# Two column states per GpSimd instruction: 128x1024 instead of 128x512 in turns 2 and 3

## The reference

```python
def step(state, xs):
    d_t, B_t, C_t, u_t = xs
    dA = jnp.exp(d_t[..., None] * A)
    state = state * dA + (d_t * u_t)[..., None] * B_t[:, None, :]
    y_t = jnp.einsum('ben,bn->be', state, C_t)
    return (state, y_t)
```

## Time and profile before

| | |
|---|---|
| median of 3 runs | 1370.07 us (1369.11 to 1371.49) |
| profiled execution, time | 1370.06 us |
| its span in the profile | 1368.3 us |
| TensorE busy | 1313.6 us, 96% |
| VectorE busy | 967.9 us, 71% |
| ScalarE busy | 623.3 us, 46% |
| GpSimd busy | 572.6 us, 42%, 317 instructions |
| TensorE's granted clock, mean | 0.991 of full speed |

### The profile page before, as it was taken

One profiled execution on the slowest core, in us unless ns is written; L12 is line 12 of the kernel. 1 busy time (PEld: TensorE's weight loads), 2 busy tenths in 40 slices (PEclk: granted clock), 3 DMA queues, 4 the chain that ended last, 5 costly groups with the idle time before them and its releaser, 6 DMA issues.

```text
span 1368.3 us, 17588 instructions
## 1 busy us (share of the span) xinstructions
PE 1313.6 (96%) x6018; PEld 1036.5 (76%) x6018; DVE 967.9 (71%) x1074; ACT 623.3 (46%) x1016; POOL 572.6 (42%) x317
## 2 busy tenths in 40 slices
PE   7899799999999999999999899999999899999999
PEld 4455478777777778888888778888888788888887
DVE  6899867899999776699999666699999523211111
ACT  6888366666565345544444135554443121111111
POOL 0000545788898421566765111566674211111111
PEclk8999999999999999999999999999999999999999
DMA  6211676776667755655555756555555665555552
GB/s 222 93 54 62 208 286 245 270 262 236 225 245 268 284 202 196 197 189 184 173 187 187 276 186 202 201 194 189 168 194 160 210 214 186 184 184 184 184 187 89
DMA packets 92301, 269.16 MB, mean 197 GB/s; under 512 B 11633, under 2 KB 11761, under 8 KB 91841
## 3 DMA queue, kind: packets, MB, share of 16 engines
q1 hardware_dynamic: 86912, 261.01, 55.7%
q10 hardware_dynamic: 5312, 7.16, 1.5%
HBM read 210.20 MB, written 57.93 MB: 196 GB/s over the span
## 4 chain that ended last, share of the span: by engine, by line
PE 76%; DVE 15%; issue 6%; ACT 2%; DMA 0%; DVEq 0%; ACTq 0%; POOL 0%
PE ps_hg L526 24%; PE ps_h L526 21%; PE ps_y L526 15%; DVE st L1278 8%; PE ps_y L707 8%; PE ps_mid L605 4%; DVE st L1269 2%; DVE y_rows L1289 2%; PE ps_mid L567 1%; PE ps_mid L526 1%; PE ps_y L549 1%; ACT dA L932 0%; DVE acc L1435 0%; DMA in_w<-in_in_wT_dram 0%; PE ps_mid L582 0%
## 5 line engine op out<-in xcount | busy, mean ns | idle before, releaser
L1597 POOL TENSOR_TENSOR h_lo<-h_tmp,h_hi 128x512 fp32r<-128x512 f32 x128 | 238.0, 1863 | 520.5 <-ACT h_hi L1007 458.2
L526 PE MATMUL ps_h<-x_hi,w_split 128*128 128x512 f32 x1024 | 344.9, 399 | 1.6 <-ACT x_hi L969 0.9
L526 PE MATMUL ps_hg<-x_hi,wg_split 128*128 128x512 f32 x1024 | 342.2, 395 | 0.6 <-DVE h_tmp L1442 0.6
L1278 DVE TENSOR_TENSOR_SCAN st<-dA,st 128x1024 f32<-128x1024 f32 x128 | 325.0, 2549 | 0.0
L1442 DVE TENSOR_TENSOR h_tmp<-h_tmp,ps_hg 128x512 f32<-128x512 f32 x128 | 88.1, 688 | 283.9 <-PE ps_hg L526 281.4
L526 PE MATMUL ps_y<-w_split,h_hi 128*128 128x512 f32 x1024 | 254.5, 396 | 0.0
L1007 ACT ACTIVATE h_hi<-h_tmp 128x512 fp32r<-128x512 f32 x128 | 80.6, 630 | 328.7 <-DVE h_tmp L1442 328.7
L526 PEld LDWEIGHTS ps_h<-x_hi,w_split 128*128 128x128 f32 x1024 | 193.2, 189 | 42.8 <-issue 2.9
L526 PEld LDWEIGHTS ps_hg<-x_hi,wg_split 128*128 128x128 f32 x1024 | 192.4, 188 | 40.4 <-issue 1.0
L526 PEld LDWEIGHTS ps_y<-w_split,h_hi 128*128 128x128 f32 x1024 | 188.1, 188 | 37.6
L1001 ACT ACTIVATE h_tmp<-ps_h 128x512 f32<-128x512 f32 x128 | 76.2, 595 | 293.2 <-PE ps_h L526 291.7
(11 more groups left out here) (161 smaller groups left out, 1298.6 us busy)
## 6 DMA issues: line engine op xcount, KB each, us to landing
w_split<-split_scratch SPq DMA_DIRECT2D x192, 512.0 KB, 5.5
wg_split<-split_scratch SPq DMA_DIRECT2D x96, 512.0 KB, 4.6
split_scratch<-w_split SPq DMA_DIRECT2D x64, 512.0 KB, 4.5
b_all<-xd_scratch SPq DMA_DIRECT2D x64, 256.0 KB, 4.1
split_scratch<-wg_split SPq DMA_DIRECT2D x32, 512.0 KB, 3.0
w_raw<-in_W_dram SPq DMA_DIRECT2D x14, 1024.0 KB, 7.4
wg_raw<-in_Wg_dram SPq DMA_DIRECT2D x7, 1024.0 KB, 9.4
dA<-in_x_dram SPq DMA_DIRECT2D x4, 1024.0 KB, 8.5
```

Of the source, the lines that this page charges most:

```text
L526: mm = pe.matmul(out_, lhs[a], rhs[c], start=first and q == 0, stop=last and q == len(sides) - 1)
L1278: dve.tensor_tensor_scan(flat[1], flat[0], flat[1], 0.0, ALU.mult, ALU.add).then_inc(scan_done, 1)
L1597: pool.tensor_tensor(h_lo[:, j, :], h_tmp[j % 2][:], h_hi[:, j, :].bitcast(F32), ALU.subtract).then_inc(hl_ready, 1)
```

## The change

In `column_state`, the two 128x512 multiplies of a part become one of 128x1024, with C's row repeated over the two tiles by a broadcast access pattern, and the two adds become one of 128x1024. The semaphores rise by 2 per instruction rather than by 1 twice. The waits on GpSimd's own semaphores are for the whole part.

```diff
                 used, odd = NC * (m - 2) + k, COLS[k] % 2
                 pool.wait_ge(cc_ld[used % 2], 16 * (used // 2 + 1))
                 pool.wait_ge(scan_done, 2 * (DS * m + COLS[k]) + part // 2 + 1)
-                for et in (part, part + 1):
-                    pool.tensor_tensor(st[odd][:, et, :], st[odd][:, et, :], c_all[used % 2], ALU.mult).then_inc(col_scaled, 1)
+                two = slice(part, part + 2)
+                by = c_all[used % 2].rearrange("p (a l) -> p a l", a=1).broadcast_to([P, 2, L])
+                pool.tensor_tensor(st[odd][:, two], st[odd][:, two], by, ALU.mult).then_inc(col_scaled, 2)
                 pool.wait_ge(ud_ready, T * m)
-                for et in (part, part + 1):
-                    pool.wait_ge(col_scaled, T * used + et + 1)
-                    if k:
-                        pool.wait_ge(col_added, T * (used - 1) + et + 1)
-                    pool.tensor_tensor(y_cols[:, et, :], y_cols[:, et, :], st[odd][:, et, :], ALU.add).then_inc(col_added, 1)
+                pool.wait_ge(col_scaled, T * used + part + 2)
+                if k:
+                    pool.wait_ge(col_added, T * (used - 1) + part + 2)
+                pool.tensor_tensor(y_cols[:, two], y_cols[:, two], st[odd][:, two], ALU.add).then_inc(col_added, 2)
```

## The result

The changed kernel takes 1405.57 us (median of 4 runs, 1404.92 to 1406.31); the kernel before, 1370.24 on the same chip. The ratio is 1.0258, with a 95% interval of 1.024 to 1.0276: 35.3 us slower. The sign was forecast, and the hold-up is there; but the 1389.5 us forecast account for 19.4 of the 35.3 us only, and the range ended at 1393.

A forecast was written before the change was run, and what follows sets the result against it. TensorE sets the pace in the column steps, with VectorE under 3 us to spare. Two turns of 1.81 + 4 x 1.97 us add 19.4 to 1370.06, forecast 1389.5 us; range 1369 to 1393.

The forecast's parts named there:

- the hold-up: Column part 2: GpSimd's longer multiply keeps out VectorE's scan (line 1278), which ends 1.97 us later, and TensorE waits.
- Length of the new instruction: GpSimd's 128x1024 column instruction: about 2.37 us, from 2 x 1.29 - 0.20.
- the fixed cost of 0.20: Cost of each GpSimd instruction whatever its size, gone 40 times: 0.20 us each, 8 us beside other work.
- Part 0 at the end of the step: GpSimd's column part 0 meets VectorE's multiply and scan at the end of a step: VectorE 0.91 us late.
- The wait with shorter cover: GpSimd's add waits for the multiply directly in front of it: 0 us taken, 0.1 us without cover.
- The tie: Column part 2: GpSimd's multiply can begin at 653.01, VectorE asks for its scan at 653.03; GpSimd first by 0.02 us.
- The first rival: At column part 2 VectorE's scan comes before GpSimd's multiply in eight steps: +1.6, 1371.7 us; chance 0.20.
- The third h_tmp is reached in time ... lateness isn't handed on to the next step.: VectorE's third h_tmp of a step, due at 661.18, is reached with 0.48 us to spare; each step pays anew.
- the cover of 1.43 us: VectorE's idleness of 1.43 us before h_tmp takes up its lateness, so the scan is asked for as before.
- Sum: Column steps of two turns: 2 x (1.81 + 4 x 1.97) = 19.4 us on 1370.06, thus 1389.5 us.

The follow-up runs named there:

- part 0 alone: Only part 0 of each column uses 128x1024 instructions, against the kernel before: 1379.99 us, ratio 1.0079.
- memset run: The changed kernel with a 128x1 memset on GpSimd in front of each column's part 2: 1374.05 us, ratio 1.0025 to the kernel before.
- run with long multiplies alone: Only the multiplies are 128x1024, the adds stay 128x512, against the kernel before: 1373.09 us, ratio 1.0014.
- run that kept TensorE busy: The changed kernel with ten unread matmuls of 512 columns before the first transposes of each column step: 1392.04 us, ratio 1.0154 to the kernel before.
- part 2 alone: Only part 2 of each column uses 128x1024 instructions, against the kernel before: 1384.3 us, ratio 1.0101.

## Why the prediction was wrong

- *Length of the new instruction.* 2.37 us taken, 2.38 to 2.40 measured. Right, and with it the fixed cost of 0.20.
- *Part 0 at the end of the step.* Right: VectorE late by 0.90 us (its multiply is taken up 0.18 us ahead of h_lo, 614.47 against 614.65, where it was 1.08 before), 0.91 forecast. The first half of the change alone shows where it goes, from the idleness in front of line 1442 (0.53 and 0.54 us left of 1.43) into h_lo.
- *The wait with shorter cover.* Priced at 0 behind cover: right. Its own size was 0.23 and not 0.1 us.
- *The tie.* Called for GpSimd by 0.02 us, and so it was. This was luck. By the prediction's own arithmetic a length of 2.38 to 2.45 us lets the scan come first, and 2.38 to 2.40 was measured; GpSimd was first by 0.02 all the same. In the first step of a turn the margin was 0.07 and not 0.18. Only the fourth column step of turn 2 was no tie: VectorE asked for its scan 0.7 us later there, and the scan took 3.87 us. The memset run turned it by 0.06 us, and the run with long multiplies alone fell on the other side with the same instruction lengths in that place. The first rival is real; it had 0.20.
- *The hold-up.* 1.97 us per step; TensorE waited 2.66 in the longest case against 0.66, thus 2.0. In all 19.8 us by the waits, 20.4 by the traces and 21.8 by the medians of the run that kept TensorE busy; 19.4 forecast. Right.
- *"The third h_tmp is reached in time ... lateness isn't handed on to the next step."* Right over the turn: in the run with TensorE kept busy the scans of turn 2 that TensorE waits for lie 39.35, 39.40, 40.13 and 38.77 us apart, 157.65 in all against 149.62 before, thus 2.0 per step. TensorE's transposes behind them lie evenly, 39.41, 39.48 and 39.39 apart from the second step on. The fourth scan was asked for 0.7 us later, since VectorE was behind there (no idleness left in front of line 1442, where the other steps have 0.53), but it then took 3.88 and not 4.53 us and ended as if on time. So in that step the cover of 1.43 us was used up; what made VectorE later was not followed up. The third h_tmp had 0.39 us of idleness left in the second and third step.
- **The step that failed: "Sum".** It took every product of TensorE behind the stall at the length that it had before. Rows 5 showed 0.66 us of idleness with the clock full; nothing in the rows told that at 2.6 it stays full, and the range had no term for it. What the runs show in its place: in the trace of the changed kernel the clock falls to half behind the stall in nine of the ten steps (all but the first of turn 2), and once more behind the columns of turn 2. A step is then 40.98 and not 39.40 us, 1.58 more; nine times, 14.2 us. The granted clock of 0.87 over the 13 us from 772 adds up to 1.7 us, worked out as 13 x 0.13. With the waits' 19.8 that makes 35.7, against 35.5 measured from the first column to the end of the span, and 35.3 by the medians. Why the clock falls behind one such gap and not behind another stays open.

## What to carry to other kernels

Before making a GpSimd instruction longer, look at which two-input VectorE instruction is asked for while it runs, and who waits for that one: the price is the rest of the longer instruction, and GpSimd's own busy time says nothing about it. A long instruction elsewhere can still cost, when it makes VectorE late and so shifts who comes first at that place (part 0 alone: 9.7 us). If two engines reach such a shared resource within 0.1 us of each other, neither order is a forecast; fix the order with a wait, which here turned 35 us of loss into 1.9 of gain. And when a change makes TensorE idle longer at a place that comes back in every step, as here from 0.66 to 2.6 us, price the matmuls behind the gap at the lower clock too, as a bound: here 3.94 us for a product of 2.76.

## What was not expected of the hardware

- TensorE's clock fell after gaps of 1.91 and 2.64 us in the midst of dense matmuls, and twelve matmuls behind such a gap took 3.94 us instead of 2.76. By the traces this cost 15.1 us, three quarters of what the gaps themselves did (20.4). The same gap didn't always do it: in the changed kernel 2.58 us left it at 1.00 in turn 2 and took it to 0.67 in turn 3. Gaps of 1.51 us, which the kernel before has too without any fall, took it down once with part 2 alone and once in the changed kernel (777 us).
- It falls at the same point of each following step of a turn: the scans of 616.80 and 657.78 in the changed kernel are 40.98 us apart, and so are the stretches of lower clock behind them. No run tried whether a step of another length would break this.
- An instruction of 0.1 us on GpSimd moved the one behind it by 0.06 us, and by this the kernel's time by 31.5 us.
